# Moving the last block's first two expert layers, for half of the tokens, in among the last causal heads

## The chip, the cores and the metric

The kernel runs on one core of a Trainium2 chip. The metric is the device time of one execution in microseconds. Six transformer sub-layers are computed in one launch; the time shown is that of the whole launch.

## What is computed

`x` has 8 batches of 112 tokens with 256 channels. Block 0 is linear attention, cross attention and a routed expert layer; block 1 is a Taylor-feature attention, cross attention with a softmax over 375 context rows, and a last sub-layer that has a causal attention and four experts. After each sub-layer comes a residual sum and a layer norm. The change lies in the last sub-layer:

```python
h = _rms(x, n1_w)
q = _rms(heads(wq), qn_w); k = _rms(heads(wk), kn_w); v = heads(wv)     # 16 heads of 16
attn = softmax(causal(q @ k^T * HD ** (-0.5)))
ao = (attn @ v) @ wo.T;  ao[:, :, :64] = 0;  x = x + ao
xf = _rms(x, n2_w).reshape(-1, C)                                       # 896 tokens x 256
wts = top-2 of softmax(xf @ gate_w.T), renormalized, over 4 experts
o0 = _gelu(xf @ e0_up.T) @ e0_down.T
o1 = silu(xf @ e1_w1.T) * (xf @ e1_w2.T) @ e1_down.T
o2 = _gelu(_gelu(_gelu(xf @ e2_l1.T) @ e2_l2.T) @ e2_l3.T) @ e2_l4.T
o3 = _gelu(_gelu(xf @ e3_down.T) @ e3_up.T) @ e3_out.T
return x + (wts[:, 0:1] * o0 + ... + wts[:, 3:4] * o3)                  # first 64 channels 0
```

## The kernel before, in words

**Stages and orders.** The program has six stages. In each, a planner writes one list of units, `plans[stage]`, and every engine then runs its own part of each unit in the order of that list. `weave` goes round the streams of a stage (generators) and takes one unit of each in turn. A stream holds back with `until(units)` (those must be placed), with `rest(ns)` (so much planned time, `spent`, must go by; each kind of unit adds its `cost`) or with `until_banks(count)`, which needs `count + 3` of the six shared PSUM banks whose release is already planned. If every stream holds back in a row, `hurry` ends the rests. Engines wait on each other by counters: T (TensorE, PE), A (ScalarE, ACT), V (VectorE, DVE), G (GpSimd, POOL). Each stage begins with `fence`: an engine waits until all four counters have reached the end of the stage before.

**Stage 4** (`plans[4]`, from L2058) holds the cross attention of block 1 (`sc4`, `tr4`, `av4`, `out`) and, woven into it batch by batch, the causal attention (names with a 5): `rms5a`, `qkv5` (projections), `qkv5e` (square, copy of q and k, copy of v on ACT), `ms5` (DVE sum, then a power on POOL), `qk5` (DVE scales q and k, L2671), `qkT5` and `qkT5e` (turned, q on ACT, k on DVE), then for each group g of four heads `s5` (scores of two groups, PE L2532 and the mask L2535, in two banks), `mx5` (DVE maximum, L2686), `s5e` (four exps on ACT, L2619), `pT5` (turned on PE L2541, copied on DVE L2691), `av5` (L2551), and per batch `oT5`, `turn5`, `atT5`, `wo5`, `sqb5`, `msb5` (power on POOL), `xf5`, `xfT5`, and `xfT5e`, which leaves the normalized tokens as two float16 parts in `xf16`. "s5 7.0" below means unit `s5` of batch 7, first pair of groups; "exps 6.1" means `s5e` of batch 6, group 1. Batches 6 and 7 are the last; nothing of the cross attention is left by then to fill between their steps. Even and odd batches are streams of their own. Banks 0 to 5 (`w4`) are shared by all of this; a new tenant takes the bank whose release was planned first.

The weights of the experts are loaded by DMA in `ffnin`, once the cross attention's last `av4` is done. `split5(name)` turns a float32 weight into two float16 parts, the first on ACT (L2579), the second on DVE (L2584). The stream `s5_split` places three such splits late in stage 4: `e0_up` after `qkT5e` of batch 7, `e1_w1` and `e1_w2` after the last exps.

**Stage 5 of the list** (`plans[5]`, functions `tensor_s6` and so on) holds the experts. Tokens are taken in halves of 448 (`hf` 0 is batches 0 to 3). `ly` is one tile of 128 outputs of a layer with gelu: 6 products of 448 columns for `e0_up` (two contraction tiles, three pairs of float16 parts), gelu on ACT (L2923), copy to float16 on ACT (L2926), the remainder on POOL (L3043). `gt` is one tile of the gated expert: `e1_w1` and `e1_w2` (6 products each, in two banks), silu on ACT (L2933), product with the gate on DVE (L3007), copy on ACT (L2936), remainder on POOL. `ax` multiplies the hidden tiles with the last layer's weights (12 products of 192 columns) and adds them on DVE with the routing weight (L3015). `gate6`, `r6` 0 to 21 and `exp6` compute the routing: 32 small float32 products on PE, then a chain of some 22 steps on DVE with one exp on ACT after step 4. Four banks serve `ly` and `gt` (`up6`), four serve `ax` and `gate6` (`misc6`). The first sum needs step `r6` 21. Four streams are woven: the experts, the routing, nine more splits, and the first final norms; in the first rounds each expert unit is followed by one step of the routing and one split. The experts stream begins:

```python
for hf in range(2):
    yield from s6_layer("e0_up", hf)     # 4 units "ly" each
for hf in range(2):
    yield from s6_gated(hf)              # 4 units "gt" each
for e in range(2):
    for hf in range(2):
        yield from s6_add(e, hf)         # 4 units "ax" each, after r6 21
```

Of the kernel before, what the change touches and what calls it, by code (L numbers as in the profile page):

```python
# [156 lines left out]
def build(nc, ctx, a, out):  # L157
# [1917 lines left out]
    for group, things in zip(ffn_groups, (  # L2075
# [5 lines left out]
        for name, shape in things:  # L2081
# [73 lines left out]
              "oT5", "turn5", "atT5", "atT5e", "wo5", "sqb5", "msb5", "xf5", "xfT5", "xfT5e", "split5")  # L2155
    w16 = {}
# [145 lines left out]
    def s5_split():  # L2302
        yield from until(("qkT5e", B - 1))
        yield split5(w16_m, "e0_up")
        yield from until(("s5e", B - 1, 3))
        yield split5(w16_m, "e1_w1")
        yield split5(w16_m, "e1_w2")

    for b in range(B):
        L_k4get[b % 2].plan(("k4get", b))  # L2310
    for m in range(2 * B):
# [6 lines left out]
          s5_split())  # L2318
    end_stage()

    def tensor_s4():
        fence(pe, 4)
        for unit in plans[4]:
# [40 lines left out]
            elif what == "out":  # L2364
# [3 lines left out]
                   [(s4_attT[:, k, :], Wo4[:, k, :]) for k in range(HW // P)], T.up("out", 4, b))  # L2368
            elif what in UNITS5:
                tensor_s5(what, at, unit)  # L2370
            else:
                tensor_ends(what, at, unit)

    def scalar_s4():
        fence(act, 4)
        for unit in plans[4]:
# [22 lines left out]
            elif what == "oT4":  # L2399
                b, q = at  # L2400
                if b:
# [4 lines left out]
                              ACT.Copy).then_inc(*A.up("oT4", b, q))  # L2406
            elif what in UNITS5:
# [4 lines left out]
    def vector_s4():  # L2412
        fence(dve, 4)
        for unit in plans[4]:
# [30 lines left out]
            elif what == "out":  # L2445
                s, b = at
                vector_add(4, b, 0, res, G["bias", 4, b], rings["misc4"][unit][0:N, 0:D])
            elif what in UNITS5:
# [4 lines left out]
    def gpsimd_s4():  # L2453
        fence(pool, 4)
        for what, *at in plans[4]:
            if what == "out":
                gpsimd_pow(*at)
            elif what == "n15":
                pool.wait_ge(g_w5.ready)
                for name in ("wq5", "wk5", "wv5"):  # L2460
                    for c in range(KC):
                        w = ffn_w[name][:, c, :]
                        GP.tensor_scalar(w, w, ch("n1", c), None, ALU.mult).then_inc(
                            *(G.up("n15") if (name, c) == ("wv5", KC - 1) else G.up()))
            elif what in UNITS5:
# [251 lines left out]
    def gpsimd_s5(what, at):  # L2717
# [25 lines left out]
        elif what == "xfT5e":  # L2743
# [3 lines left out]


# [4 lines left out]
    ring6 = Region(nc, ringm.base, 46 * KB)  # L2753
# [11 lines left out]
    hidden = [ring6.tensor(f"hidden{i}", [P, 2, HT, HALF], F16)[:] for i in range(5)]  # L2765
    raw5 = [ring6.tensor(f"raw5_{i}", [P, HALF])[:] for i in range(4)]
    rings.update(up6=banks(0, 4), misc6=banks(4, 4), hidden=Ring(hidden), raw5=Ring(raw5))
# [4 lines left out]
    step("ly", "T ly, A gelu, A lh, G ll", "up6", "A gelu", 1500)  # L2772
    step("gt", "T gt1, T gt2, A silu6, V gate6, A gh, G gl", "up6", "A silu6", 3000)
# [440 lines left out]
```

## Time and profile before

| what | us |
|---|---|
| median of 3 runs | 1302.74 (1296.62 to 1307.76) |
| profiled execution, its own time | 1312.95 |
| its span, first to last instruction | 1311.1 |
| PE busy in the span | 1073.4 (82%) |
| DVE, ACT, POOL busy | 660.0, 579.7, 276.5 |

The profile is of one execution. Busy shares are means over stages with different limits. "PEclk" is the clock that was granted to TensorE: 1.00 is 2.4 GHz, 0.50 is 1.2 GHz, values between are mixes over the stretch. In a timeline the bracket at the end of a line is the idle time of the engine before it and what ended it. L378 is the helper `mm`, in which all plain products are issued, so its rows are told apart by their tiles (`e_up`, `e_w`, `e_down`).

### The profile page before, as it was taken

To read this page: it belongs to the slowest core of one execution; us is meant where nothing else is said; L and a number is where in the kernel's file an instruction comes from. 1 tells how busy PE (TensorE), PEld (TensorE's weight loads), DVE (VectorE), ACT (ScalarE), POOL (GpSimd) and SP (SyncE) were. 2 spreads that over 40 slices of the span, in tenths; PEclk is the share of its full clock that TensorE was granted. 3 is DMA by queue.
4 is the path that set the end of the run, shared out by engine and by line. 5 is a ranking of instruction groups with operands and counts; after the bars stand their busy time and mean duration, and the time that the engine had idled before them with its cause. 6 is when DMAs were issued, how large, how long until landed. Compare 5 with 4: busy or idle time off the path is not lost.

```text
span 1311.1 us, 20866 instructions
## 1 busy us (share of the span) xinstructions
PE 1073.4 (82%) x8272; PEld 770.2 (59%) x8272; DVE 660.0 (50%) x1614; ACT 579.7 (44%) x1357; POOL 276.5 (21%) x282
## 2 busy tenths in 40 slices
PE   6988678876775877778999978898988888777996
PEld 3677446665543877644556546675766666544754
DVE  3422356641382677335445543776677766435103
ACT  4411136544124566233445433555546555456542
POOL 2410212200022000042111120032022222323543
PEclk9876768979778999888999988997999999668998
DMA  9320225600158476164222215433231204000000
GB/s 308 90 42 0 77 43 113 141 19 2 48 171 265 167 269 242 37 204 132 83 85 78 83 47 165 125 95 94 72 95 38 82 24 161 40 0 1 1 1 29
DMA packets 66593, 123.62 MB, mean 94 GB/s; under 512 B 11537, under 2 KB 42225, under 8 KB 62417
## 3 DMA queue, kind: packets, MB, share of 16 engines
q1 hardware_dynamic: 63728, 117.48, 29.3%
q0 software_dynamic: 1536, 3.67, 0.9%
q8 instruction: 65, 1.06, 0.4%
q10 hardware_dynamic: 1232, 1.15, 0.3%
q14 instruction: 32, 0.25, 0.1%
HBM read 86.30 MB, written 35.92 MB: 93 GB/s over the span
## 4 chain that ended last, share of the span: by engine, by line
PE 59%; DVE 20%; ACT 10%; DMA 4%; POOL 3%; issue 3%; SPq 1%; another core or an unknown queue 0%; DVEq 0%; ACTq 0%
PE psum L378 43%; ACT s_p L2396 2%; DVE s_p L2444 2%; POOL rs L2733 2%; DVE s_max L1258 2%; DVE s_max L2433 2%; DMA values<-s_v 2%; PE psum L1115 2%; PE psum L1143 2%; PE psum L2348 2%; PE psum L2359 2%; PE psum L2532 1%; DVE wu L1088 1%; DVE wd L1088 1%; DVE s_pT L2425 1%
## 5 line engine op out<-in xcount | busy, mean ns | idle before, releaser
L2396 ACT ACTIVATE s_p<-psum,s_max 112x375 f32<-112x375 f32 x128 | 72.1, 568 | 87.6 <-DVE s_max L2433 87.6
L601 POOL TENSOR_TENSOR rstd<-meanvar,minus_half 112x1 f32<-112x1 f32 x40 | 22.8, 570 | 347.7 <-DVE meanvar L582 347.6
L1258 DVE TENSOR_REDUCE s_max<-psum 112x2 f32<-112x750 f32 x64 | 60.0, 937 | 41.1 <-PE psum L1115 40.2
L378 PE MATMUL psum<-Wv,ctx 128*125 128x512 f16 x240 | 64.2, 429 | 9.8 <-ACT s_v L561 5.4
L378 PE MATMUL psum<-ctx,Wk 128*128 128x375 f16 x320 | 64.2, 337 | 5.0 <-ACT s_yT L1971 2.8
L2733 POOL TENSOR_TENSOR rs<-ms,minus_half 112x32 f32<-112x32 f32 x8 | 43.5, 5440 | 111.1 <-DVE ms L2667 111.1
L2433 DVE TENSOR_REDUCE s_max<-psum 112x1 f32<-112x375 f32 x128 | 63.7, 539 | 1.0 <-PE psum L2340 0.9
L2348 PE MATMUL psum<-ident,s_p 112*125 112x112 f32 x384 | 60.2, 291 | 4.3 <-DVE s_p L2444 3.0
L1207 ACT ACTIVATE s_pT<-psum 125x672 f32<-125x672 f32 x64 | 46.7, 730 | 36.2 <-PE psum L1131 34.8
L561 ACT ACTIVATE s_v<-psum 125x512 f32<-125x512 f32 x48 | 28.5, 596 | 75.3 <-PE psum L378 48.8
L3043 POOL TENSOR_TENSOR hidden<-raw,hidden 128x448 f16<-128x448 f32 x44 | 45.5, 1035 | 65.8 <-ACT hidden L2926 64.1
L553 ACT ACTIVATE s_k<-psum 128x375 f16<-128x375 f32 x64 | 31.2, 487 | 63.2 <-PE psum L378 61.1
L2340 PE MATMUL psum<-s_k,s_q 64*112 64x375 f16 x384 | 45.5, 342 | 16.6 <-ACT s_p L2396 5.9
L378 PE MATMUL psum<-wd,hid 128*70 128x256 f16 x384 | 45.9, 282 | 16.0 <-DVE hid L1684 16.0
L2348 PEld LDWEIGHTS psum<-ident,s_p 112*125 112x125 f32 x384 | 50.6, 194 | 13.4 <-DVE s_p L2444 4.7
L1115 PE MATMUL psum<-s_kd,s_qd 48*112 48x375 f16 x128 | 27.8, 429 | 36.9 <-DVE s_max L1258 28.3
L2359 PE MATMUL psum<-s_pT,s_v 125*64 125x112 f32 x768 | 53.6, 277 | 4.4 <-ACT s_attT L2404 4.4
L378 PEld LDWEIGHTS psum<-Wv,ctx 128*125 128x125 f16 x240 | 35.8, 154 | 35.7 <-issue 11.8
L378 PEld LDWEIGHTS psum<-wd,hid 128*70 128x70 f16 x384 | 43.1, 117 | 18.0 <-DVE hid L1684 17.3
L591 DVE SCALAR_TENSOR_TENSOR s_k<-psum,s_k 128x375 f16<-128x375 f32 x64 | 34.8, 546 | 37.1 <-ACT s_k L553 36.7
L2359 PEld LDWEIGHTS psum<-s_pT,s_v 125*64 125x64 f32 x768 | 39.6, 143 | 20.8 <-issue 18.0
L378 PE MATMUL psum<-x_ch,w_Wq 128*128 128x224 f32 x192 | 49.1, 400 | 1.8 <-ACT x_ch L567 1.0
(353 smaller groups left out, 2556.1 us busy)
## 6 DMA issues: line engine op xcount, KB each, us to landing
keys<-s_k SPq DMA_DIRECT2D x64, 187.5 KB, 2.2
s_k<-keys SPq DMA_DIRECT2D x8, 1500.0 KB, 7.1
values<-s_v SPq DMA_DIRECT2D x48, 224.0 KB
s_v<-values SPq DMA_DIRECT2D x16, 672.0 KB
raw_wg<-in_wg SPq DMA_DIRECT2D x8, 1024.0 KB
raw_wu<-in_wu SPq DMA_DIRECT2D x8, 1024.0 KB, 6.0
raw_wd<-in_wd SPq DMA_DIRECT2D x8, 1024.0 KB, 5.7
s_kd<-k_halves SPq DMA_DIRECT2D x48, 93.8 KB, 3.9
```

The source lines that it names most:

```text
L378: ins = TE.matmul(bank, left, right, start=i == 0, stop=last)
L591: VE.scalar_tensor_tensor(t[:, 1, :], rings["misc3"][unit][:, 0:S], 1 / WSCALE, t[:, 0, :], ALU.mult, ALU.subtract).then_inc(*V.up("k4", *at))
L1115: ins = TE.matmul(bank[0:N, j, 0:S], s1_qd[b // 2 % 2][rows, p, b % 2, :], s1_kd[b % 3][rows, p, :], start=True, stop=True)
L1207: SC.activation(rings["pT1"][n], rings["t1"][unit][0:SCH, :, 0:NCH * N], ACT.Exp, scale=0.25).then_inc(*A.up("exp1", n))
L1258: VE.tensor_reduce(s1_max[b % 2][:, 2 * p:2 * p + 2], rings["s1"][unit][0:N, :, 0:S], X, ALU.max, negate=True).then_inc(*V.up("max1", n))
L2340: ins = TE.matmul(rings["s4"][(n, j)][0:N, 0:S], q[rows, p, u, cols(b % 2)], k[rows, p, v, :], start=i == 0, stop=i == 2)
L2348: ins = TE.transpose(rings["t4"][unit][0:SCH, c * N:(c + 1) * N], p[:, c * SCH:(c + 1) * SCH], ident[0:N, 0:N])
L2359: ins = TE.matmul(rings["o4"][n // 4][64 * j:64 * j + 64, p % 4 * N:(p % 4 + 1) * N], s4_v[n // 4 % 3][:, c, 2 * (p % 4) + j, :], rings["p ...
L2396: SC.activation(rings["p4"][2 * n + j], rings["s4"][(n, j)][0:N, 0:S], ACT.Exp, bias=s4_max[b % 2][:, h:h + 1], accum_out=s4_sum[b % 2][:, ...
L2433: VE.tensor_reduce(s4_max[b % 2][:, h:h + 1], rings["s4"][(n, j)][0:N, 0:S], X, ALU.max, negate=True).then_inc(*V.up(name, n))
L2733: GP.tensor_tensor(rs5[b % 2][:], ms5[b % 2][:], minus_half[:], ALU.pow).then_inc(*G.up("rs5", b))
L3043: GP.tensor_tensor(dst[:, 1, f, :], raw_, dst[:, 0, f, :], ALU.subtract).then_inc(*G.up("ll", *at))
```

## The change

The eight units of the first half of the tokens (`ly` of `e0_up`, `gt` of `e1`) are placed in stage 4 by the stream `s6_first`, which takes the place of `s5_split`. They use the six banks of `w4`, which the heads use. The split of `e0_up` is placed once batch 7's input is turned (`xTe`), its four `ly` from `qkv5e` of batch 7 on, then the two splits of `e1`; the four `gt` start after the first scores of batch 7 are placed. The stage of the experts starts with the second half. The bodies of `ly` and `gt` on each engine become functions that both stages call; ACT gets one more wait (the last `out` of the cross attention), since `hidden` lies over memory that is used until then. `hidden` and `raw5` get fixed places that are free in both stages.

```diff
-    def s5_split():
-        yield from until(("qkT5e", B - 1))
+    def s6_layer(name, hf, shared=False):
+        yield from until(("split5", name))
+        take_hidden(name, hf)
+        for f in range(tiles_of(name)):
+            if shared:
+                yield from until_banks(1)
+            rings["raw5"].take((name, hf, f), (G, ("ll", name, hf, f)))
+            yield [("ly", name, hf, f)]
+
+    def s6_gated(hf, shared=False):
+        yield from until(("split5", "e1_w1"), ("split5", "e1_w2"))
+        take_hidden("e1", hf)
+        for f in range(HT):
+            if shared:
+                yield from until_banks(2)
+            rings["raw5"].take(("e1", hf, f), (G, ("gl", hf, f)))
+            units = [("gt", hf, f)]
+            yield units
+            rings["up6"].take(("gtb", hf, f), (V, ("gate6", hf, f)))
+
+    def s6_first():
+
+        yield from until(("xTe", 4, B - 1))
         yield split5(w16_m, "e0_up")
-        yield from until(("s5e", B - 1, 3))
+        yield from until(("qkv5e", B - 1))
+        yield from s6_layer("e0_up", 0, True)
         yield split5(w16_m, "e1_w1")
         yield split5(w16_m, "e1_w2")
+        yield from until(("s5", B - 1, 0))
+        yield from s6_gated(0, True)
...
-          s5_split())
+          s6_first())
...
+            elif what in ("ly", "gt"):
+                tensor_layers(what, at, unit)
...
+    def up_ring(unit):
+
+        return w4 if unit in w4.by_key else rings["up6"]
...
+    def scalar_layers(what, at, unit):
+        act.wait_ge(T["out", 4, B - 1])
+        if what == "ly":
+            name, hf, f = at
+            raw_, dst = rings["raw5"][name, hf, f], rings["hidden"][name, hf]
+            if f == 0:
+                act.wait_ge(*rings["hidden"].free((name, hf)))
+            act.wait_ge(T["ly", *at], *rings["raw5"].free((name, hf, f)))
+            SC.activation(raw_, up_ring(unit)[unit][:, 0:HALF], ACT.Gelu,
+                          scale=1 / WSCALE).then_inc(*A.up("gelu", *at))
+            act.wait_ge(A["gelu", *at])
+            SC.activation(dst[:, 0, f, :], raw_, ACT.Copy).then_inc(*A.up("lh", *at))
...
     def s6_experts():
-        for hf in range(2):
-            yield from s6_layer("e0_up", hf)
-        for hf in range(2):
-            yield from s6_gated(hf)
+        yield from s6_layer("e0_up", 1)
+        yield from s6_gated(1)
         for e in range(2):
```

## Rows read from the trace of the kernel before

**Rows 1.** The page, chain that ended last, share of the span by engine.
```profile
PE 59%; DVE 20%; ACT 10%; DMA 4%; POOL 3%; issue 3%; SPq 1%; another core or an unknown queue 0%; DVEq 0%; ACTq 0%
```

**Rows 2.** Timeline of PE, 1138 to 1224 us: start, us, engine, line, operation, count.
```profile
1138.25 1.84 PE L2532 MATMUL psum<-k,q 32*112 32x224 f32 x8 [1.94 <-ACT e_up L2579]
...
1151.86 0.59 PE L2551 MATMUL psum<-pT,v 112*32 112x112 f32 x16 [2.10 <-DVE pT L2691]
...
1161.99 2.40 PE L378 MATMUL psum<-xf,e_up 128*128 128x448 f16 x6 [1.89 <-POOL xf L2745]
1164.19 6.00 PE L378 MATMUL psum<-w_gate,xf 128*112 128x4 f32 x32
...
1180.43 3.57 PE L378 MATMUL psum<-xf,e_w 128*128 128x448 f16 x18
...
1192.69 15.17 PE L378 MATMUL psum<-xf,e_w 128*128 128x448 f16 x72 [2.06 <-ACT raw L2933]
1207.70 16.26 PE L378 MATMUL psum<-e_down,hidden 128*112 128x192 f16 x192
```

**Rows 3.** Stretches: us; busy (count) PE, PEld, DVE, ACT, POOL; PEclk, DMA share, GB/s.
```profile
1100.00:1150.00 50.00, 38.22 (x257) 27.43 (x252) 22.76 (x49) 22.78 (x73) 16.39 (x11) 0.76 0.33 132
1150.00:1200.00 50.00, 36.02 (x166) 20.31 (x167) 21.79 (x42) 31.12 (x51) 15.05 (x17) 0.73 0.00 1
```

**Rows 4.** Timelines of DVE and of POOL, columns as in rows 2.
```profile
1132.34 0.68 DVE L2671 TENSOR_TENSOR qk<-qk,rs 112x512 f32<-112x512 f32 x1
...
1208.51 0.16 DVE L2976 CAST ek<-top_i 112x8 f32<-112x8 uint32 x1
...
1211.33 1.39 DVE L3015 SCALAR_TENSOR_TENSOR x_tok<-psum,wt,x_tok 112x192 f32<-112x192 f32 x4
...
1125.02 5.43 POOL L2733 TENSOR_TENSOR rs<-ms,minus_half 112x32 f32<-112x32 f32 x1 [6.01 <-DVE ms L2667]
```

**Rows 5.** Busy time by short stretch, columns as in rows 3.
```profile
1128.00:1130.00 2.00, 0.60 (x4) 0.38 (x4) 0.62 (x1) 1.30 (x6) 2.00 (x1) 1.00 0.00 0
1146.00:1150.00 4.00, 3.76 (x37) 3.18 (x35) 2.87 (x6) 3.10 (x10) 0.00 (x0) 0.78 0.00 0
1154.00:1158.00 4.00, 2.63 (x8) 1.73 (x8) 1.10 (x4) 1.64 (x5) 1.61 (x3) 0.57 0.00 0
```

**Rows 6.** Timeline of ACT, columns as in rows 2.
```profile
1126.25 3.04 ACT L2619 ACTIVATE sc<-psum,mx 112x112 f32<-112x112 f32 x12 [2.36 <-DVE mx L2686]
...
1184.63 1.89 ACT L2579 ACTIVATE e_l<-w_e_l 128x2048 f16<-128x2048 f32 x1
1186.54 1.28 ACT L2923 ACT_TABLE_LOAD   x1
1187.83 0.54 ACT L2923 ACTIVATE raw<-psum 128x448 f32<-128x448 f32 x1
1188.41 0.58 ACT L2926 ACTIVATE hidden<-raw 128x448 f16<-128x448 f32 x1
...
1197.23 0.53 ACT L2933 ACTIVATE raw<-psum 128x448 f32<-128x448 f32 x1
...
1198.93 0.52 ACT L2933 ACTIVATE raw<-psum 128x448 f32<-128x448 f32 x1
```

**Rows 7.** DMA issues 1095 to 1125 us: KB each, median us from issue to landing.
```profile
w_e_w<-in_e_w SPq DMA_DIRECT2D x2, 512.0 KB, 4.9
```

**Rows 8.** The page, groups of instructions: busy, mean ns, idle before.
```profile
L3043 POOL TENSOR_TENSOR hidden<-raw,hidden 128x448 f16<-128x448 f32 x44 | 45.5, 1035 | 65.8 <-ACT hidden L2926 64.1
```

**Rows 9.** Groups by line and form, ACT, 1100 to 1225 us, columns as in rows 8.
```profile
L2579 ACT ACTIVATE e_w<-w_e_w 128x1024 f16<-128x1024 f32 x2 | 2.0, 1072 | 0.0
```

**Rows 10.** Groups by line and form, DVE, 1130 to 1225 us.
```profile
L2584 DVE SCALAR_TENSOR_TENSOR e_l<-w_e_l,e_l 128x2048 f16<-128x2048 f32 x2 | 4.6, 2292 | 5.0 <-ACT e_l L2579 5.0
L2691 DVE COPY pT<-psum 112x448 f32<-112x448 f32 x7 | 4.3, 620 | 1.6 <-PE psum L2541 1.6
...
L3001 DVE FIND_INDEX8 top_i<-top,pr 112x8 uint32<-112x8 f32 x8 | 1.1, 160 | 0.0
```

More of the change, by code:

```diff
@@ L2155, in build @@
               "oT5", "turn5", "atT5", "atT5e", "wo5", "sqb5", "msb5", "xf5", "xfT5", "xfT5e", "split5")
+    step("ly", "T ly, A gelu, A lh, G ll", "up6", "A gelu", 1500)
+    step("gt", "T gt1, T gt2, A silu6, V gate6, A gh, G gl", "up6", "A silu6", 3000)
+    hidden_m = Region(nc, ringm.base, 35 * KB)
+    hidden = [hidden_m.tensor(f"hidden{i}", [P, 2, HT, HALF], F16)[:] for i in range(5)]
+    spare = Region(nc, wts.base + 46 * KB, 5 * KB), Region(nc, ringm.base + 36 * KB + 512, 3 * KB + 512)
+    assert wts.at <= 46 * KB and ringm.at <= 36 * KB + 512
+    raw5 = [spare[i // 2].tensor(f"raw5_{i}", [P, HALF])[:] for i in range(4)]
+    rings.update(up6=w4, hidden=Ring(hidden), raw5=Ring(raw5))
     w16 = {}
@@ L2406, in scalar_s4 @@
                               ACT.Copy).then_inc(*A.up("oT4", b, q))
+            elif what in ("ly", "gt"):
+                scalar_layers(what, at, unit)
             elif what in UNITS5:
@@ L2746, in gpsimd_s5, with product6, x_half, tensor_layers @@
                              ALU.subtract).then_inc(*G.up("xf16", b))
+    def product6(bank, name, f, src, kt, mark):
+        pe.wait_ge(V["w5", name])
+        mm(bank[:, 0:HALF], [(w16[name][:, u, k, f * P:(f + 1) * P], src[:, v, k, :])
+                             for k in range(kt) for u, v in PARTS], mark)
+    def x_half(hf):
+        return xf16[:, :, :, hf * HALF:(hf + 1) * HALF]
+    def up_ring(unit):
+        return w4 if unit in w4.by_key else rings["up6"]
+    def tensor_layers(what, at, unit):
+        if what == "ly":
+            name, hf, f = at
+            src = BEFORE.get(name)
+            if src:
+                pe.wait_ge(G["ll", src, hf, tiles_of(src) - 1])
+            else:
+                pe.wait_ge(G["xf16", hf * 4 + 3])
+            pe.wait_ge(*up_ring(unit).free(unit))
+            product6(up_ring(unit)[unit], name, f, rings["hidden"][src, hf] if src else x_half(hf),
+                     ffn_w[name].shape[1], T.up("ly", *at))
+        elif what == "gt":
+            hf, f = at
+            pe.wait_ge(*up_ring(unit).free(unit))
+            product6(up_ring(unit)[unit], "e1_w1", f, x_half(hf), KC, T.up("gt1", *at))
+            pe.wait_ge(*up_ring(unit).free(("gtb", hf, f)))
+            product6(up_ring(unit)[("gtb", hf, f)], "e1_w2", f, x_half(hf), KC, T.up("gt2", *at))
```

141 lines of the change are left out of this document (53 added, 88 removed).

## The prediction

> **What bounds the kernel now.** I read the page first, then the table by stretches, then the chain, then the timeline of each engine between 1095 and 1230 us. The chain that ended last is mostly TensorE [rows 1], but not evenly. From 1207.70 us on the expert layers of the last block run with hardly a gap on PE: the first products with `e0_down` start there [rows 2], and nothing of the change touches what follows, 1311.1 - 1207.7 = 103.4 us. Before that lie two weaker stretches. In 1100 to 1200 us PE is busy 38.22 and 36.02 of 50 us at a granted clock of 0.76 and 0.73, while ACT is busy 22.78 and 31.12 [rows 3]. The first half is the tail of the causal heads, where batch 7 goes from engine to engine: the power on GpSimd takes 5.43 us and scaling q and k starts at 1132.34 [rows 4], the first scores of batch 7 start at 1138.25, the last of its head outputs at 1151.86, and the first expert layer at 1161.99 [rows 2]. The clock drops to 1.2 GHz after PE idled (1128 to 1130: 0.60 of 2.00 us busy), is back at 2.4 within 1146 to 1150 and drops again within 1154 to 1158 [rows 5]; the first tile of the experts still takes 2.40 us for 6 products, later ones 3.57 for 18 [rows 2]. The second half is the front of the expert stage: eight tiles of `e0_up`, eight gated pairs and the gate's 32 small products, 1207.70 - 1161.99 = 45.7 us.
>
> **What the change moves.** For tokens 0 to 447 it moves four `ly` (24 products) and four `gt` (48 products) from the front into the tail. PE has room: at 2.4 GHz 18 products take 3.57 us and 72 take 15.17 [rows 2], so a `ly` is 1.2 us and a `gt` 2.4, and 72 products are some 14 us of PE. Whether that is a gain depends on the in-order queues they are put into, ACT's above all, so I walk the planner.
>
> **The new order.** The stream `s6_first` is the last of the round, `ly` adds 1500 to the planned time and `gt` 3000, and the free-bank condition leaves room for `ly` beside one open pair of scores (2 of 6 banks) and for `gt` only when at most one bank is held. This gives on PE: qkv5 7, wo5 5, ly 0, s5 6.0, ly 1, ly 2, ly 3, s5 6.1, pT5 6.0, pT5 6.1, pT5 6.2, av5 6.0, pT5 6.3, xfT5 5, av5 6.1, qkT5 7, s5 7.0, turn5 6, gt 0, atT5 6, s5 7.1, pT5 7.0, gt 1, pT5 7.1, wo5 6, gt 2, pT5 7.2, av5 7.0, gt 3, pT5 7.3, av5 7.1, then the tail as before. On ACT: gelu 0, sqb5 5, gelu 1, gelu 2, exp 6.0, gelu 3, split of e1_w1, exp 6.1, split of e1_w2, exp 6.2, exp 6.3, oT5 6, xf 5, q5 7, exp 7.0, silu 0, exp 7.1, at 6, exp 7.2, silu 1, silu 2, exp 7.3, silu 3, sqb5 6, oT5 7. Gelu, exp and silu each need their own table: the front shows a load in every turn between them, 1.28 us each [rows 6]. The order has nine such turns in the tail, where before there was none; in the front there are five before and five after. Nine loads are 11.5 us of ACT, four gelus with their copies 4 x 1.12 = 4.5 (0.54 + 0.58), and a silu with its gate and copy takes 1.70 from one to the next (1197.23 to 1198.93) [rows 6], 6.8 for four.
>
> **No cost.** The DMAs of the weights are issued at 1100.64 and land in 4.9 us [rows 7], the first split would read them at about 1118. The three splits are the same instructions on ACT and DVE, one of them moved ahead by some 19 us and two by 12 to 15; SP gets nothing new. The GpSimd subtractions (1.03 us each [rows 8]) go around the 5.43 us power: one ahead of it, about 1 us, covered because the scaling of q and k now waits for something later (next paragraph); uncovered it would be 1 us.
>
> **Tail, first part.** ly 0 fits at 1123 beside the wait for the scores and ends at 1124.2. From there ACT has: load 1.28, gelu 1.12, square 0.5, two gelus 2.24, load 1.28, exps 6.0 1.03, load 1.28, gelu 1.12, split 1.07 [rows 9], load 1.28, exps 6.1 1.03: 13.2 us, so exps 6.1 end at about 1137.4. Before, twelve exps of that batch (6.0 to 6.2) ran from 1126.25 to 1129.3 without a load [rows 6], about 1.03 for four. The planner puts qk5 7 behind the copy of pT5 6.1 on DVE, and DVE has before it the second split (ready at 1138.4, 1.2), two copies (0.62 each [rows 10]), a maximum of the same size and xf5 5 (some 2 in all). So the scaling starts near 1141, 8.5 us later than 1132.34. From it to the first scores 5.9 us as before (1132.34 to 1138.25): s5 7.0 at about 1147.
>
> **Tail, second part.** Before, s5 7.0 to av5 7.1 took 1151.86 - 1138.25 = 13.6 us. Now ACT has from the start of exps 7.0, 2.6 us after s5 7.0: four exps 4.2, five loads 6.4, four gates 6.8, the small copies and the square 0.9, and about 2.5 of waiting for turn5 6 and gt 0 on PE at 1.2 GHz: 20.8, so av5 7.1 comes 23.4 us after s5 7.0, at 1170.4. That is 18.5 later than before; with 10.1 us to the first expert layer (1151.86 to 1161.99), unchanged, the front starts at 1180.5.
>
> **Front.** PE has 2.40 for the first tile, 6.0 for the gate's products, three tiles and four gated pairs, 23 us in all. But the sums with the routing weights wait for the routing chain on DVE, which the planner interleaves one step per expert unit; with half the units its second half stands behind the last splits. ACT from the second tile's end (10 us in): three gelus with their copies and three splits, by columns from [rows 9], 5.8, load 1.28, three gates with two splits 7.0, load and exp of the routing 1.5, split of 2048 columns 1.89, load 1.28, last gate 1.7, split 1.89: 32.4 us in. With some 0.7 for waits between them that is 33. Then DVE's 2.29 for that split [rows 10] and half as much for the last, and the chain from its eighth step to the end: 2.8 for the last nine steps (1208.51 to 1211.33 [rows 4]) and an estimated 2.5 for the maxima, the index searches (160 ns each [rows 10]) and four small steps. In all 33 + 2.3 + 1.15 + 2.8 + 2.5 = 41.8 us in, the first sum: 1222.3, against 1211.33 before [rows 4]. PE can run four of the `e0_down` products ahead into four banks, then stands, and goes on at 1222.7 where it was at 1211.7. Front: from its first tile to the first sum 49.3 us before, 41.8 now, 7.5 less.
>
> **Sum.** +18.5 - 7.5 = +11.0 us; what PE saves in the front (72 products) beyond the 7.5 is lost in that wait. The profiled execution was 1312.95 us (span 1311.1), so this one would be 1324. The median of the runs shown is 1302.74, 0.8% less; the same stretches carried over give 1314. A measurement of this kernel tells about 1% (13 us) from no change, so this is just inside.
>
> **What is not in the trace.** How the clock stands in the new tail. With all of it at 2.4 GHz the same walk gives the front's end 1 us earlier than now (-1), with all of it from 1130 us at 1.2 GHz some 37 later. I take the pattern of before, a drop after idle time near 1131 and one after 1168, and dense `gt` products to bring it back; those are the nearest rows [rows 5], and they lie in between. PE's new wait of some 12 us before the fifth `e0_down` product may lower the clock once more, 1 to 3 us, not in the sum.
>
> **A rule of the Trainium skill.** The load itself is 1.28 us here; at 1186.54 it starts where the split before it ended (1184.63 + 1.89) and the gelu follows at 1187.83 [rows 6], so a turn costs 1.29. The Trainium skill, ScalarE: Activation LUTs, section "What ACT_TABLE_LOAD costs", gives 1.28 us for the load and 1.38 more for a drain, 2.66 for each switch. By that figure the nine turns would be an estimated 24 us instead of 11.6 and the forecast 12 us worse; the trace of the front speaks against it. The same page says to batch functions by table set, which this order does not.
>
> **Rivals.** (1) The tail is not held up: ACT was busy only 22.78 of 50 us [rows 3], the order leaves exps near their old places, and the front still starts at 1162. For it: PE's and ACT's gaps. Against: batch 6's exps stand in the queue behind four gelus and three loads. Then the routing chain, 41.8 us in, decides: 1203.8 against 1211.3, -7.5 us, 1295. It holds once av5 7.1 starts by about 1155; the earnings of the front then exceed the delay. To win over 1% the chain would have to be shorter too, ax starting right after the gates: 45.7 - 23 = 22.7 less, 1280. (2) PE's clock stays low through most of the tail: gaps between heads are longer than before because ACT is later. For it: the drops in [rows 5] came after 2 us of idle time. Against: the moved products are long. Half way between my pattern and all low: +24, 1327. (3) A turn of tables costs twice what its row shows where work is in flight: nine times 1.28 more on ACT, +11.5, 1325. (4) It changes nothing: at 2.4 GHz throughout, tail and front cancel (-1), 1302.
>
> **Chances.** Forecast 0.50, rival 1 0.15 (half of it the large gain), rival 2 0.15, rival 3 0.05, rival 4 0.15. Forecast's own range 1308 to 1321. Faster by over 1%: 0.08; slower by over 1%: rivals 2 and 3 and over a third of the forecast, 0.38; the rest 0.54. Range 1293 to 1327.
>
> **What would show it.** Right: 17 table loads instead of 8; exps 6.1 near 1137, s5 7.0 near 1147, av5 7.1 near 1170, first tile of the second half near 1180; PE idle some 12 us after four `e0_down` products, ended by a sum on DVE, and from the fifth product some 99 us to the end (1311.1 - 1211.7) as before. Wrong: s5 7.0 before 1141 (ACT hides the loads), or a front that ends without that wait (the chain of routing is not the bound), or clock 1.0 from 1130 on.

## The result, and the profile after

| kernel | median, us | ratio to before (95%) |
|---|---|---|
| before | 1302.36 (14 runs) | |
| after | 1314.05 (14 runs) | 1.0087 (1.0063 to 1.0111) |

The change makes the kernel 11.3 us slower by the ratio (8.2 to 14.5); 1314 was predicted. (The medians are of all runs; the ratios, here and below, leave out executions that fell in a slower state, so they are not exactly the quotients of the medians.) The profiled execution of after took 1316.46 us, its span is 1314.6, only 3.5 more than the span of before. That difference misleads: the part ahead of the change, which both kernels have alike, took 1104.28 us in the profiled execution of before and 1092.34 in this one, up to the start of the last product of the cross attention (`out` of batch 7, on PE the product of `w_Wo` and `s_attT`). In the twelve other profiled kernels it took 1084 to 1108. So I put all traces on top of each other at the start of that product, and give times as "us in" from there. From it to the end, before takes 206.8 us and after 222.3: +15.4.

Not all of that is the change's. These are lines of the timeline of PE in before, then in after, columns as in [rows 2]:

```profile
1104.28 3.62 PE L378 MATMUL psum<-w_Wo,s_attT 128*112 128x256 f32 x16
...
1120.41 1.04 PE L378 MATMUL psum<-w_wk,x_ch 128*112 128x256 f32 x4
```
```profile
1092.34 3.62 PE L378 MATMUL psum<-w_Wo,s_attT 128*112 128x256 f32 x16
...
1108.47 1.91 PE L378 MATMUL psum<-w_wk,x_ch 128*112 128x256 f32 x4
```

The second line of each, a projection of batch 7, starts 16.1 us in and stands ahead of the first moved unit. In before the granted clock is 1.00 from 16.4 us in on (1120.70 to 1122.70); in after it is still 0.50 up to 18.4 (1108.76 to 1110.76), and the next unit, `wo5` of batch 5, starts 19.4 us in instead of 17.9. The profiled executions of e5, e6 and e9 below, which leave the heads as they were, show the same late return of the clock, with s5 7.0 at 35.2 us in instead of 34.0. So 1.2 to 1.5 us of the 15.4 are a difference that also stands between executions without the change. (All seven profiled kernels with units among the heads have the late return, and three of the seven others; whether the order makes it likelier is open.)

| us in | before | predicted | after |
|---|---|---|---|
| exps 6.1 end | | 33.1 | 34.7 |
| qk5 7 starts (DVE) | 28.1 | 36.7 | 38.7 |
| s5 7.0 | 34.0 | 42.7 | 45.0 |
| av5 7.1 | 47.6 | 66.1 | 67.3 |
| first expert layer of stage 5 | 57.7 | 76.2 | 78.3 |
| first sum with the routing weights | 107.05 | 118.0 | 120.8 |
| fifth `e0_down` product | 107.4 | 118.4 | 121.4 |
| first product of `e3_down` | 119.5 | | 135.1 |
| end | 206.8 | 217.8 | 222.3 |

The page of after, the busy times and the chain by engine, answering to [rows 1]:

```profile
PE 1071.0 (81%) x8272; PEld 770.7 (59%) x8272; DVE 657.7 (50%) x1614; ACT 592.2 (45%) x1366; POOL 277.8 (21%) x282
...
PE 59%; DVE 20%; ACT 11%; issue 3%; DMA 3%; POOL 3%; SPq 0%; DVEq 0%; ACTq 0%
```

The shares of the chain hardly move, and PE has the same 8272 products. The one visible difference is ACT: 9 instructions more (1357 before) and 12.5 us busier (579.7 before). Nine loads of 1.28 us are 11.5 of them.

The timeline of PE in after, columns as in [rows 2]:

```profile
1137.31 1.84 PE L2585 MATMUL psum<-k,q 32*112 32x224 f32 x8 [1.90 <-DVE k L2730]
...
1159.65 0.98 PE L2604 MATMUL psum<-pT,v 112*32 112x112 f32 x16 [2.45 <-DVE pT L2744]
...
1170.62 2.40 PE L378 MATMUL psum<-xf,e_up 128*128 128x448 f16 x6 [1.89 <-POOL xf L2798]
1172.81 6.00 PE L378 MATMUL psum<-w_gate,xf 128*112 128x4 f32 x32
1178.67 5.83 PE L378 MATMUL psum<-xf,e_up 128*128 128x448 f16 x18
1184.34 7.02 PE L378 MATMUL psum<-xf,e_w 128*128 128x448 f16 x36
1191.56 2.67 PE L378 MATMUL psum<-xf,e_w 128*128 128x448 f16 x12 [0.20 <-ACT raw L2849]
1194.07 4.12 PE L378 MATMUL psum<-e_down,hidden 128*112 128x192 f16 x48
1213.69 13.87 PE L378 MATMUL psum<-e_down,hidden 128*112 128x192 f16 x144 [15.50 <-DVE x_tok L3063]
```

The first two lines, s5 7.0 and av5 7.1, are 22.3 us apart where [rows 2] have 13.6. From the third line to the fifth product are 43.1 us, with a stop of 15.50 us that before does not have, ended by the first sum (`x_tok` on DVE). The timeline of ACT shows what the units cost among the heads:

```profile
1118.24 0.58 ACT L2842 ACTIVATE hidden<-raw 128x448 f16<-128x448 f32 x1
1118.83 1.28 ACT L2672 ACT_TABLE_LOAD   x1
1120.13 1.09 ACT L2672 ACTIVATE sc<-psum,mx 112x112 f32<-112x112 f32 x4
1121.23 1.28 ACT L2839 ACT_TABLE_LOAD   x1
1122.53 0.54 ACT L2839 ACTIVATE raw<-psum 128x448 f32<-128x448 f32 x1
1123.10 0.58 ACT L2842 ACTIVATE hidden<-raw 128x448 f16<-128x448 f32 x1
1123.59 1.04 ACT L2632 ACTIVATE e_w<-w_e_w 128x1024 f16<-128x1024 f32 x1
1124.64 1.28 ACT L2672 ACT_TABLE_LOAD   x1
1125.94 1.09 ACT L2672 ACTIVATE sc<-psum,mx 112x112 f32<-112x112 f32 x4
```

Behind the copy of gelu 2 stand exps 6.0, gelu 3, the first split of `e1` and exps 6.1, in the order worked out from the planner. In [rows 6] twelve exps stand in 3.04 us; here two groups of four start 5.8 us apart. What ends the stop is on DVE:

```profile
1205.19 2.29 DVE L2637 SCALAR_TENSOR_TENSOR e_l<-w_e_l,e_l 128x2048 f16<-128x2048 f32 x1 [2.35 <-ACT e_l L2632]
1207.40 0.20 DVE L3014 RECIPROCAL sm<-sm 112x8 f32<-112x8 f32 x1
1207.51 0.91 DVE L2637 SCALAR_TENSOR_TENSOR e_l<-w_e_l,e_l 128x768 f16<-128x768 f32 x1
...
1212.82 0.19 DVE L3024 TENSOR_TENSOR wt<-wt,tp 112x32 f32<-112x32 f32 x1
1213.12 1.39 DVE L3063 SCALAR_TENSOR_TENSOR x_tok<-psum,wt,x_tok 112x192 f32<-112x192 f32 x4
```

The second half of the routing chain stands behind the last splits, and those behind ACT's. PE's clock in four short stretches of after, columns as in [rows 3]:

```profile
1142.00:1146.00 4.00, 4.00 (x27) 2.45 (x25) 1.39 (x3) 2.59 (x4) 0.62 (x1) 0.96 0.00 0
...
1170.00:1174.00 4.00, 3.38 (x13) 2.25 (x14) 0.15 (x2) 0.88 (x1) 0.47 (x1) 0.50 0.00 0
...
1202.00:1206.00 4.00, 0.00 (x0) 0.00 (x0) 1.65 (x4) 3.20 (x4) 1.03 (x1) 0.50 0.01 2
1214.00:1218.00 4.00, 4.00 (x31) 4.00 (x30) 1.24 (x4) 0.00 (x0) 0.00 (x0) 0.57 0.02 4
```

The third is inside the stop: no product, and the granted clock is down to 0.50 (1.2 GHz). It is still at 0.57 when the sums have begun, so the 144 products behind the stop take 13.87 us, where a share of 144 in 192 of the 16.26 us of [rows 2] is 12.2.

### The profile page after: what moved, and what is told of

Read it like the earlier page. It is cut to its first block, busy times and chain, and to the rows that moved or that the text cites. A ratio compares the mean times of both kernels' runs of the same rounds, so it can differ in the third digit from the quotient of the medians.

```text
span 1314.6 us, 20873 instructions
## 1 busy us (share of the span) xinstructions
PE 1071.0 (81%) x8272; PEld 770.7 (59%) x8272; DVE 657.7 (50%) x1614; ACT 592.2 (45%) x1366; POOL 277.8 (21%) x282
## 4 chain that ended last, share of the span: by engine, by line
PE 59%; DVE 20%; ACT 11%; issue 3%; DMA 3%; POOL 3%; SPq 0%; DVEq 0%; ACTq 0%
PE psum L378 43%; ACT s_p L2443 2%; DVE s_p L2493 2%; DVE s_max L1258 2%; PE psum L1143 2%; DVE s_max L2482 2%; DMA values<-s_v 2%; PE psum L1115 2%; POOL rs L2786 2%; PE psum L2404 2%; PE psum L2393 2%; DVE wu L1088 1%; PE psum L2585 1%; DVE wd L1088 1%; DVE s_pT L2474 1%
## 5 line engine op out<-in xcount | busy, mean ns | idle before, releaser
L378 PE MATMUL psum<-Wv,ctx 128*125 128x512 f16 x240 | 58.1, 400 | 5.8 <-ACT s_v L561 3.1
L2385 PE MATMUL psum<-s_k,s_q 64*112 64x375 f16 x384 | 45.0, 338 | 17.9 <-ACT s_p L2443 7.0
L2393 PEld LDWEIGHTS psum<-ident,s_p 112*125 112x125 f32 x384 | 49.9, 192 | 13.8 <-DVE s_p L2493 4.7
L3063 DVE SCALAR_TENSOR_TENSOR x_tok<-psum,wt,x_tok 112x192 f32<-112x192 f32 x32 | 13.1, 416 | 75.5 <-PE psum L378 75.4
L2493 DVE TENSOR_SCALAR s_p<-s_p,s_sum 112x375 f32<-112x375 f32 x128 | 49.3, 427 | 2.3
```

The lines of the kernel that those rows point to most:

```text
L378: ins = TE.matmul(bank, left, right, start=i == 0, stop=last)
L2385: ins = TE.matmul(rings["s4"][(n, j)][0:N, 0:S], q[rows, p, u, cols(b % 2)], k[rows, p, v, :], start=i == 0, stop=i == 2)
L2393: ins = TE.transpose(rings["t4"][unit][0:SCH, c * N:(c + 1) * N], p[:, c * SCH:(c + 1) * SCH], ident[0:N, 0:N])
L2493: VE.tensor_scalar(t, t, sums[:, j:j + 1], None, ALU.mult).then_inc(*V.up(name, n))
```

## The experiments

All ratios are to before on the same chip; before had a median of 1299.02 us beside e1 to e4, 1307.1 beside e5 to e8, 1302.47 beside e9 to e11, 1308.38 beside e12. A ratio has an interval of 0.2 to 0.5% on either side, mostly 4 us; the trace places a cost more finely, but two executions of the same instructions differ in it by up to 2 us in this part, too, by the moment at which the clock changes (s5 7.0 at 34.0 or 35.2 us in where nothing ahead of it was edited, stage 5 at 67.1 in e4 and 69.0 in e6). Two recorded expectations, of e7 and e10, use times of after that are counted from 1093.64 us, inside the product of `w_Wo`, and are 1.3 us too short: the 6.0, 6.2 and 14.2 us in the one are 7.3, 7.5 and 15.4, the 66.0 and 77.0 in the other 67.3 and 78.3.

| | edit | us in: s5 7.0 | av5 7.1 | stage 5 | first `e0_down` | `e3_down` | end | ratio (95%) |
|---|---|---|---|---|---|---|---|---|
| before | | 34.0 | 47.6 | 57.7 | 103.4 | 119.5 | 206.8 | 1 |
| after | | 45.0 | 67.3 | 78.3 | 101.7 | 135.1 | 222.3 | 1.0087 (1.0063 to 1.0111) |
| e1 | no tables | 41.2 | 60.2 | 70.2 | 93.9 | 127.7 | 215.0 | 1.0040 (1.0009 to 1.0071) |
| e2 | routing early | 45.0 | 67.3 | 78.3 | 103.3 | 127.5 | 214.8 | 1.0051 (1.0016 to 1.0086) |
| e3 | `ly` only | 45.9 | 57.1 | 67.0 | 108.8 | 127.7 | 215.0 | 1.0070 (1.0041 to 1.0099) |
| e4 | late place | 34.0 | 47.6 | 67.1 | 90.8 | 124.6 | 211.9 | 1.0035 (0.9996 to 1.0075) |
| e5 | before, routing early | 35.2 | 48.9 | 59.4 | 107.2 | 123.1 | 210.5 | 1.0055 (1.0023 to 1.0087) |
| e6 | late, routing early | 35.2 | 49.7 | 69.0 | 93.5 | 117.4 | 204.7 | 0.9984 (0.9952 to 1.0017) |
| e7 | no tables, routing early | 41.2 | 60.2 | 70.2 | 95.4 | 118.5 | 205.8 | 0.9976 (0.9946 to 1.0006) |
| e8 | splits after s5 7.0 | 41.4 | 66.5 | 77.1 | 100.8 | 134.6 | 221.8 | 1.0108 (1.0058 to 1.0158) |
| e9 | e6, splits last | 35.2 | 49.7 | 69.0 | 93.5 | 113.5 | 205.3 | 0.9987 (0.9954 to 1.0019) |
| e10 | e2, splits last | 45.0 | 67.3 | 78.3 | 103.3 | 121.7 | 213.0 | 1.0068 (1.0039 to 1.0098) |
| e11 | before, splits last | 34.0 | 47.6 | 57.8 | 100.0 | 116.1 | 206.1 | 0.9980 (0.9949 to 1.0012) |
| e12 | e9, splits after 6 sums | 34.0 | 47.7 | 67.2 | 92.4 | 111.9 | 199.2 | 0.9966 (0.9946 to 0.9986) |

**e1, the moved units without tables of their own.**

```diff
-                          up_ring(unit)[unit][:, 0:HALF], ACT.Gelu,
+                          up_ring(unit)[unit][:, 0:HALF], ACT.Copy if unit in w4.by_key else ACT.Gelu,
...
-                          up_ring(unit)[unit][:, 0:HALF], ACT.Silu,
+                          up_ring(unit)[unit][:, 0:HALF], ACT.Copy if unit in w4.by_key else ACT.Silu,
```

> The changed kernel with a plain copy in place of gelu and silu in the eight moved units (their values differ from the reference's). The nine table loads of the tail go, all else keeps its place. Loads hold up the tail: ACT has 11.5 us less in its queue, exps 6.1 end some 3.8 us earlier after the projections of batch 7, av5 7.1 some 10 us earlier, the first expert tile of the second half comes 9 to 11 us earlier, and the ratio to the kernel before falls from 1.009 to about 1.000 to 1.002. Rival, the places in ACT's queue and the gates' waits hold it up, not the tables: 2 to 4 us less, ratio 1.006 or more.

Measured: 1306.46 us, 1.0040; 7.3 us less in the trace, 6 by the ratios, between the theory and its rival. Of the 11.5 us of loads some 60% stood on the path. The loads are all gone from the tail, but exps 6.1 come only 4.3 us earlier (they end 30.4 us in), because batch 6's exps still stand behind the copies in the gelus' place and the splits, and qk5 7 starts 3.8 us earlier, at 34.9. Two timelines of e1, DVE and POOL, show what waits now:

```profile
1113.61 1.67 DVE L2637 SCALAR_TENSOR_TENSOR e_w<-w_e_w,e_w 128x1024 f16<-128x1024 f32 x1 [5.39 <-ACT e_w L2632]
1115.20 0.61 DVE L2739 TENSOR_REDUCE mx<-psum 112x4 f32<-112x448 f32 x1
1115.73 1.52 DVE L2637 SCALAR_TENSOR_TENSOR e_w<-w_e_w,e_w 128x1024 f16<-128x1024 f32 x1
...
1119.03 0.68 DVE L2724 TENSOR_TENSOR qk<-qk,rs 112x512 f32<-112x512 f32 x1
```
```profile
1107.76 5.43 POOL L2786 TENSOR_TENSOR rs<-ms,minus_half 112x32 f32<-112x32 f32 x1
1113.17 3.01 POOL L2866 TENSOR_TENSOR hidden<-raw,hidden 128x448 f16<-128x448 f32 x2
1116.13 1.52 POOL L2790 TENSOR_TENSOR rstd<-meanvar,minus_half 112x1 f32<-112x1 f32 x1
```

The power that qk5 7 needs (`rs`) is ready at 1113.19, the scaling starts 5.84 us later, behind two splits and the maxima and copies of batch 6. So the order of the units holds batch 7 up, not the tables alone. (The two splits are slower here than in after, by 0.7 us together; this is taken up at the end.)

**e2, the routing chain early**: as many steps of it per round as in before come with twice the units, and the last three splits wait for it.

```diff
         yield [("gate6",)]
-        for n in range(5):
-            yield [("r6", n)]
-        yield [("exp6",)]
-        for n in range(5, 22):
-            yield [("r6x8" if n in (8, 9) else "r6", n)]
+        yield [("r6", 0), ("r6", 1)]
+        yield [("r6", 2), ("r6", 3)]
+        yield [("r6", 4), ("exp6",)]
+        for n in range(5, 22, 4):
+            yield [("r6x8" if m in (8, 9) else "r6", m) for m in range(n, min(n + 4, 22))]
...
             for name in names:
+                if name == "e2_l2":
+                    yield from until(("r6", 21))
                 yield split5(region, name)
```

> The changed kernel with the routing chain placed in two, then four steps per expert unit, its exp between the last gelu and the first silu, and the three last splits after the chain. The chain of routing costs the wait at the fifth e0_down product: PE's wait of 15.5 us shrinks to under 5, the time falls 10 to 12 us, ratio about 1.000. Rival, the wait is only slack that another wait takes over (gates on ACT and DVE): under 4 us less, ratio 1.006 or more.

Measured: 1306.43 us, 1.0051; 7.5 us less in the trace, some 5 by the ratios, again between the two. Up to stage 5 this trace and that of after are alike (45.0, 67.3, 78.3), so all of it is gained behind the start of stage 5. The stop shrinks to 5.14 us, and 0.30 after one more product. It is now a split that stands ahead of the sum: in the timeline of DVE the chain ends at 1199.51, and then come

```profile
1200.18 2.29 DVE L2637 SCALAR_TENSOR_TENSOR e_l<-w_e_l,e_l 128x2048 f16<-128x2048 f32 x1 [0.68 <-ACT e_l L2632]
1202.39 0.41 DVE L3065 SCALAR_TENSOR_TENSOR x_tok<-psum,wt,x_tok 112x192 f32<-112x192 f32 x1
1202.72 2.28 DVE L2637 SCALAR_TENSOR_TENSOR e_l<-w_e_l,e_l 128x2048 f16<-128x2048 f32 x1
```

**e3, only the `ly` moved.**

```diff
-        yield from until(("s5", B - 1, 0))
-        yield from s6_gated(0, True)
...
-        yield from s6_gated(1)
+        for hf in range(2):
+            yield from s6_gated(hf)
```

> Only the four gelu units are moved, the four gated ones stay with the experts. If tail delay and wait for the routing are what counts: the tail has 4 loads and 4 gelus in it, front starts 8 to 9 us late (against 18 to 19), front shorter by the four gelu units with their part at 1.2 GHz, 5 to 8 us, routing hidden behind eight gates again: ratio 1.000 to 1.003. Rival, each moved product saves its own time on PE: ratio between 1.009 and 1, that is 1.004 to 1.005.

Measured: 1308.59 us, 1.0070: slower than I had thought by more than the interval. The four `ly` alone put stage 5 off by 9.3 us (57.7 to 67.0), and the front, from there to the first `e0_down` product, takes 41.8 us instead of 45.7: it gives back 3.9. PE's stops there (four, of 0.46 to 4.50 us) are all on the gated pairs, and these have stayed:

```profile
1184.30 2.61 PE L378 MATMUL psum<-xf,e_w 128*128 128x448 f16 x12 [0.47 <-ACT raw L2847]
1191.41 5.16 PE L378 MATMUL psum<-xf,e_w 128*128 128x448 f16 x18 [4.50 <-ACT raw L2847]
```

The routing, too, was not hidden behind the eight gates, as the theory had it: PE stands another 2.89 us for the first sum, until 1208.91.

**e4, the units late in the tail**: the `ly` and the `gt` only after the last exps.

```diff
-        yield from until(("qkv5e", B - 1))
-        yield from s6_layer("e0_up", 0, True)
+        yield from until(("qkT5e", B - 1))
         yield split5(w16_m, "e1_w1")
         yield split5(w16_m, "e1_w2")
-        yield from until(("s5", B - 1, 0))
+        yield from until(("s5e", B - 1, 3))
+        yield from s6_layer("e0_up", 0, True)
         yield from s6_gated(0, True)
```

> All eight units are moved, but behind the last exps of batch 7, with the splits of e1 once q and k of batch 7 are turned. Only two loads (gelu, silu) are in the tail, none before an exp. Batch 7's heads run as in the kernel before up to the exps 7.3, then four gelus and four gates, 12 us on ACT, stand beside the last chain of 10 us, partly ahead of its steps: front starts 6 to 10 us late; the wait for the routing stays, 41.8 us after the front's start: ratio 0.998 to 1.003. Rival, all moved work delays the front by its full ACT time wherever it stands: front 18 us late, ratio 1.009.

Measured: 1308.65 us, 1.0035. Batch 7's heads are back where they were (av5 7.1 at 47.6), the tail has two table loads instead of nine, and the delay falls from 20.6 to 9.4 us at the start of stage 5 (1.2 to 1.5 of the difference is the clock's return, early here as in before). The ratio is told neither from 1 nor from after's. The stop is untouched, 15.50 us to the hundredth, as the timeline of PE in e4 shows:

```profile
1161.86 2.40 PE L378 MATMUL psum<-xf,e_up 128*128 128x448 f16 x6 [1.89 <-POOL xf L2798]
...
1185.52 4.12 PE L378 MATMUL psum<-e_down,hidden 128*112 128x192 f16 x48
1205.14 4.22 PE L378 MATMUL psum<-e_down,hidden 128*112 128x192 f16 x25 [15.50 <-DVE x_tok L3063]
```

So tail and front are two separate costs: from the start of stage 5 to the fifth `e0_down` product it is 43.3 us here and 43.1 in after.

**e5, before with the edit of e2** (the first split held back is the same, `e2_l2`).

> The kernel before, with the routing chain early and the three last splits after it, as in the run of the changed kernel with that edit. There PE was not held by the chain (first sum 0.1 us after PE could go on), so if the wait in the changed kernel came from halving the expert units, the edit does nothing here: ratio 0.998 to 1.002. Rival, the edit helps by itself, whatever stands around it (less work ahead of the last gates): ratio 0.995 or less.

Measured: 1312.53 us, 1.0055, 3.6 us more in the trace, 1.7 of them there before stage 5: a miss for both theories. With all eight `gt` in the front, the routing's exp falls between the gelus and wide splits between the gates, PE has seven stops of 0.46 to 1.82 us on ACT and DVE, and the front takes 47.8 us instead of 45.7. In these runs the early chain is worth something only where the front is short.

**e6, e4 and e2 together.**

> All eight moved units behind the last exps of batch 7, and the routing chain early. If the two costs are separate places: the front starts 9 to 10 us late as in the late run, is 20.5 us shorter up to the first e0_down product, and the wait of 15.5 us shrinks to 5 to 8: from the last product of the cross attention to the end about 202 to 205 us against 206.8, ratio 0.994 to 0.999, faster than both kernels. Rival, the wait goes to the gates and splits on ACT and DVE instead: ratio above 1.001.

Measured: 1301.91 us, 0.9984: level with before, and faster than after by about 1% (0.9984 to 1.0087). The trace has 204.7, 17.6 less than after, within the forecast. The split of 2.29 us ahead of the first sum is there as in e2 (1189.52, while the chain ended at 1188.84).

**e7, e1 and e2 together.**

> The changed kernel with plain copies in the moved units (values differ) and the routing chain early. The single edits took 6.0 and 6.2 us of the 14.2 us between the last product of the cross attention and the end. If they lie one after the other on the path they add: 2 to 3 us over the kernel before are left in the trace, ratio about 0.999 to 1.001. Rival, one hides the other: 6 us or more are left, ratio 1.004.

Measured: 1304.67 us, 0.9976; 16.5 us less than after in the trace, where e1 and e2 alone give 7.3 and 7.5. They add up, and 1.7 us more, all of it behind the fifth `e0_down` product: from there to `e3_down` e2 takes 15.0 us (112.5 to 127.5), after 13.7, e1 14.2, e7 13.8 (104.7 to 118.5), with the same products; over the last 132 of them the granted clock is 0.87 in e2 and 0.96 in e7. The loads and the routing's place together are worth the whole loss: the ratio is not told from 1.

**e8, the two splits of `e1` after s5 7.0.**

```diff
-        yield split5(w16_m, "e1_w1")
-        yield split5(w16_m, "e1_w2")
         yield from until(("s5", B - 1, 0))
+        yield split5(w16_m, "e1_w1")
+        yield split5(w16_m, "e1_w2")
```

> The changed kernel with the two splits of the gated expert placed after the first scores of batch 7, so that DVE and ACT reach the scaling of q and k of batch 7 without them. If the splits on DVE's queue ahead of that scaling hold up batch 7: first scores of batch 7 some 3 us earlier, of which the second part gives back 1 to 2 (the splits stand before the first gate), ratio 1.006 to 1.008. Rival, the tables alone set that place: first scores unmoved or later, ratio 1.009 or more.

Measured: 1323.3 us in six runs, 1.0108, not told from after's 1.0087. s5 7.0 does start 3.6 us earlier (41.4 us in), so the splits did hold it up, but av5 7.1 gains only 0.8, with 2.8 given back instead of the 1 to 2 expected: now the two splits on ACT (2.00 us at 1145.73) and DVE hold up the first `gt`, as PE's timeline shows.

```profile
1146.83 1.84 PE L2585 MATMUL psum<-k,q 32*112 32x224 f32 x8 [1.94 <-ACT e_w L2632]
...
1152.39 3.94 PE L378 MATMUL psum<-xf,e_w 128*128 128x448 f16 x12 [1.94 <-DVE e_w L2637]
```

So what the splits no longer cost ahead of s5 7.0 they cost behind it: that part is 25.2 us here and 22.3 in after.

**e9, e10, e11, the last three splits behind the sums.** The edit is one line, in e6 (e9) and in e2 (e10); in before (e11), which has no such condition, it is put in:

```diff
                 if name == "e2_l2":
-                    yield from until(("r6", 21))
+                    yield from until(("ax", 1, 1, 3))
```

> As the late run with the early routing chain, and the three last splits behind the sixteen sums instead of behind the chain. In that run the chain ended 3.3 us before PE went on, with a split of 2.29 us on DVE ahead of the first sum and another ahead of the second. If those splits held the sums: the wait falls from 7 us to about 2, the time by 4 to 6 us, from the last product of the cross attention to the end about 199 to 201 us, ratio to the kernel before 0.994 to 0.997. Rival, the splits come due later and hold the layers of the third expert instead: ratio 0.998 or more.

> The units where the change puts them, with the same front as the run beside it. Only the place of the eight units differs between the two. If the place among the heads costs what the traces say (head outputs of batch 7 at 66.0 us against 47.6, front's start 77.0 against 67.1), it stays 9 to 10 us slower than the late one, ratio 1.002 to 1.005. Rival, the longer the tail the more of it the front gives back: within 3 us of the late one.

> The kernel before with only the three last splits behind the sixteen sums. There a split of 1.89 us and a table load stood on ACT ahead of a silu while PE was idle 4.4 us, and another split ahead of the next. If the splits are part of those waits: 2 to 5 us less, ratio 0.996 to 0.999, and part of what the late run gains is not the move's. Rival, the loads alone make them, or the clock: ratio 1.000.

Measured: 1301.85 us and 0.9987; 1310.16 and 1.0068; 1302.57 and 0.9980. e9 differs from e10 only in where the eight units stand: 9.3 us at the start of stage 5 and 7.7 at the end in the traces (both have the late return of the clock), 0.8% by the ratios; the rival of within 3 us is out. In e11 the stops on the gates shrink from 4.43 and 2.06 us to 2.61 and 1.16, so the splits were part of those waits; that it is faster than before is not shown (0.9949 to 1.0012). In all three the front gets shorter (`e3_down` comes 3.9 us earlier in e9 than in e6, 5.9 in e10 than in e2, 3.4 in e11 than in before), and in all three most or all of it is lost again, as the rival of e9 has it: from `e3_down` to the end it is 91.8, 91.3 and 90.0 us, and 87.2 to 87.4 in all the others. In e9 the place is right behind `e3_down`, as the timelines of PE and of POOL show:

```profile
1210.45 4.70 PE L378 MATMUL psum<-xf,e_down 128*128 128x448 f16 x24
1218.02 10.94 PE L378 MATMUL psum<-hidden,e_up 128*128 128x448 f16 x48 [2.86 <-POOL hidden L2866]
```
```profile
1215.86 4.80 POOL L2866 TENSOR_TENSOR hidden<-raw,hidden 128x448 f16<-128x448 f32 x3 [1.69 <-ACT hidden L2842]
```

The splits now stand between the gelus of `e3_down` on ACT, and PE waits 2.86 us for its hidden tile, after which 48 products take 10.94 instead of 9.25 us.

**e12, e9 with the three splits after the sixth sum.**

```diff
                 if name == "e2_l2":
-                    yield from until(("ax", 1, 1, 3))
+                    yield from until(("ax", 0, 1, 1))
```

> The moved units late in the tail (as in e4) and the routing chain early (as in e9), but the last three splits of weights put after the sixth of the weighted sums instead of the sixteenth, so that ScalarE does them while it has nothing else and none of them stands before the gelus of the next layer. Theory (e9 lost its gain there: TensorE stood 2.86 us on a gated product and the next 48 products took 10.94 us instead of 9.25): the front is as short as in e9, 113.5 us from the last cross-attention product to the first product of the down layer of expert 1, and from there to the end it is 87.3 us again: 200.8 together against 206.8 before, a ratio to before of 0.995 (0.993 to 0.998). VectorE has the three splits (2.28, 2.28, 0.95) with only a sum between them, so TensorE may stand up to 2 us there. Rival: what the first sums earn is lost wherever the splits stand (the sums are held up behind them by as much as TensorE gained): 204 or more, ratio 0.998 to 1.000.

Measured: 1305.08 us beside 1308.38 for before, 0.9966 (0.9946 to 0.9986): 4.4 us faster than before (1.8 to 7.1), and some 1.2% faster than after. The theory holds: `e3_down` to the end is 87.3 us again, the stop between the products is 0.61 us, and the end comes 199.2 us in (1.8 us of the 6.1 to e9's end stand before stage 5, where only the clock differs). The timeline of PE in e12:

```profile
1188.31 4.12 PE L378 MATMUL psum<-e_down,hidden 128*112 128x192 f16 x48
1194.80 7.11 PE L378 MATMUL psum<-e_down,hidden 128*112 128x192 f16 x84 [2.37 <-DVE x_tok L3065]
1202.53 5.42 PE L378 MATMUL psum<-e_down,hidden 128*112 128x192 f16 x60 [0.61 <-DVE x_tok L3065]
1207.79 4.70 PE L378 MATMUL psum<-xf,e_down 128*128 128x448 f16 x24
1212.58 9.25 PE L378 MATMUL psum<-hidden,e_up 128*128 128x448 f16 x48
```

The trace's gain (7.6 us) is larger than the measured one; it is of one execution of each. How much of the 4.4 us is the move's is not shown: before with this front, the routing packed and the splits behind the sixth sum, was not run, and e11, before with only the last splits put behind the sums, is at 0.9980, not told from e12.

## Why the prediction was right

**Tail, first part.** Forecast s5 7.0 +8.7 us (1147 against 1138.25), found +11.0. The order of the units on ACT is the one worked out, and exps 6.1 end at 34.7 us in (33.1); the late return of the clock accounts for 1.2 to 1.5 us of what is over. (The step's own terms for qk5 7, 1138.4, 1.2 and some 2, give 1141.6, where it wrote "near 1141" and 8.5.) The reason given, batch 6's exps queued behind gelus and loads, is borne out by e4, where the eight units stand elsewhere and s5 7.0 is back at 34.0. The word "loads" carried too much: without them (e1) it is 41.2, so 3.8 of the 11.0 are tables, and e8 shows 3.6 for the two splits, which the step had counted, one on ACT and one on DVE.

**Tail, second part.** Forecast 23.4 us, found 22.3 (13.6 before). Tables are 3.3 of the 8.7 more (e1: 19.0); the other 5.4 stand with gates, silus and their copies in the queues, which no run takes apart.

**The ten us to stage 5.** Taken as unchanged, they grew from 10.1 to 11.0: at a lower clock av5 7.1 takes 0.98 us instead of 0.59, and the products behind it (`oT`) 1.10 instead of 0.65.

**Front.** The first sum was to come 41.8 us after the first tile; it came after 42.5 (1170.62 to 1213.12), and what bounds it is the chain behind the splits: in e2 it comes after 33.7. "PE stands some 12 us" was a slip: by the step's own terms, 23 us to the first `e0_down` product, 4 for four of them and 42.2 to the fifth, it is 15, and 15.50 was found. The sum did not use the 12.

**Sum.** Forecast +11.0 us, found 11.3 by the ratio and 15.4 between the two traces: +11.0, +8.7, +0.8, -6.6 up to the fifth product, and +1.5 behind it. Against the forecast's terms (+8.7, +9.8, 0, -7.5, 0) that is 4.4 us over, of which 1.2 to 1.5 are the clock's return. The last term is the clock after the stop, "1 to 3 us, not in the sum"; it should have been in it, as should the 0.8. So the mechanism was right, but that the ratio comes out 0.3 us from the forecast is in part luck: single terms were off by up to 2.3 us, and the ratio itself is known to 3 us.

**The rivals.** (1) The tail not held up: out, by 11.0 and 20.6 us. No run has the units in the tail and stage 5 at its old time: with the heads left as they were (e4, e12) it still starts 9.4 and 9.5 us late, since the eight units then stand behind the last exps. Its other half, that a shorter chain of routing would win, holds for the front, by 18.0 us where it named 22.7: in e12 the fifth `e0_down` product comes 31.7 us after the start of stage 5 (67.2 to 98.9) where before has 49.7. (2) Low clock through most of the tail: out: the clock is at 0.50 in pieces of the tail, but 0.96 from 1142 to 1146, and stage 5 starts 2.1 us later than forecast with the pattern of before, not the 13 that this rival adds. (3) A turn at twice its row: out. The exps start 1.30 us after the load does (1118.83, 1120.13), and the load starts 0.01 us after the copy ahead of it ends. (4) Nothing: out by the interval.

**The page of the Trainium skill.** ScalarE: Activation LUTs, "What ACT_TABLE_LOAD costs", adds 1.38 us for a drain to each switch. The traces do not agree: in all nine turns of the tail the activation starts within 1.35 us of the load's start, and with no gap ahead of the load, so the nine cost ACT some 12 us and not the estimated 24 of that figure. The same page, "Table sets: the hidden batching unit", says to batch functions by table set. e1, with the turns alone taken out, is 7.3 us shorter; e4, with two turns in the tail instead of nine, 10.4, but there the units also stand elsewhere.

What stays open: what the move by itself is worth once the front is mended (the kernel before with e12's front), and whether the units among the heads bring on the late return of the clock.

## What to carry to other kernels

Work moved into the gaps of a latency-bound stretch is not free because the engine that it is named for is idle there: it costs what it puts in front of the critical steps in every other engine's queue, here gelus, silus, table loads and splits on ScalarE ahead of the last batch's exps (the next stage starts 20.6 us later for 14 us of matmuls). Put such work behind the last critical step in each queue (7.7 us between e10 and e9), and count table turns. And when a stretch gets shorter, ask which chain was paced by its length: the routing's steps were interleaved one per unit and stood behind the splits, and the loss went away only when they were packed closer (e6), and a kernel told from before came only with the splits put where neither the sums nor the next layer's gelus wait for them (e12).

## What the hardware showed besides

Two engines slow each other down. A split of 1024 columns on VectorE takes 1.22 us alone (1128.00 in after) and 1.67 and 1.52 us in e1 while GpSimd works on the lines shown there; of the subtraction of 448 columns GpSimd does two in 3.01 us there (1.03 each in [rows 8]), and the power of one column, 0.55 us at 1100.40 in e1, takes 1.52. In e9 three subtractions beside two splits take 4.80 us. The Trainium skill, GPSIMD Engine Reference, "Key points", says that GpSimd shares its SBUF interfaces with VectorE and contends with VectorE instructions that read two SBUF inputs, as the split does; the traces agree. So a cost taken from a row of one of the two engines holds only as long as the other is idle. The prediction's 1.2 us for a split did not allow for this, which did no harm: in after the two take 1.31 and 1.22 us.

ScalarE's table load can also run ahead of what its activation waits for: in after one starts at 1205.91, and its gelu, which waits for PE, at 1228.73. So a turn costs nothing where the engine would wait anyway.
